# One-hot tiles made a step ahead, three-tile runs in the last block, and cleared-tile matmuls at the start of a DLRM tower kernel

## The reference, cut to what matters

```
e = jnp.stack([tbl_f[ids[:, f]] for f in range(39)], axis=1)      # [512, 39, 32]
p = e[:, ROW, :]; q = e[:, COL, :]                                # all pairs i < j
z = jnp.einsum('bpc,apc,bpa->bp', p, w, q)                        # [512, 741]
h = jnp.concatenate([z, dense_ctx], axis=1)
h = jnp.maximum(h @ W_top1 + b_top1, 0.0)                         # 757 -> 512
h = jnp.maximum(h @ W_top2 + b_top2, 0.0)                         # 512 -> 256
y = h @ W_top3                                                    # 256 -> 1
```

## Time and profile before

| | |
|---|---|
| time, median of three runs | 221.22 us (219.29 to 221.88) |
| time of the profiled execution | 221.21 us |
| its span, first to last instruction | 219.5 us |
| mean granted TensorE clock | 0.946 of full speed |
| TensorE busy | 194.5 us (89%), 1276 matmuls |
| VectorE busy | 143.3 us (65%), 140 instructions |
| GpSimd busy | 135.1 us (62%), gathers until 141 us |
| ScalarE busy | 41.8 us (19%) |
| transfers | 9.75 MB, nearly all in the first 28 us |

### The profile page before, as it was taken

One profiled execution on the slowest core, in us unless ns is written; L12 is line 12 of the kernel. 1 busy time (PEld: TensorE's weight loads), 2 busy tenths in 40 slices (PEclk: granted clock), 3 DMA queues, 4 the chain that ended last, 5 costly groups with the idle time before them and its releaser, 6 DMA issues.

```text
span 219.5 us, 3186 instructions
## 1 busy us (share of the span) xinstructions
PE 194.5 (89%) x1276; PEld 60.4 (28%) x1276; DVE 143.3 (65%) x140; ACT 41.8 (19%) x55; POOL 135.1 (62%) x202
## 2 busy tenths in 40 slices
PE   2599956568489999999998999999989999899895
PEld 1244512111122222232323232323322232222341
DVE  3599924743506889899967658899964566455310
ACT  3977820000020002001111021101011121101323
POOL 7998988898988888888888888600022222204000
PEclk9999996676758999999999999999999999999999
DMA  5999900000000000000000000000000000000000
GB/s 151 290 323 410 330 12 15 9 12 9 12 15 12 10 12 17 13 12 10 15 12 12 13 14 11 12 3 1 1 1 3 0 0 0 0 3 1 0 0 0
DMA packets 6682, 9.75 MB, mean 44 GB/s; under 512 B 1974, under 2 KB 4470, under 8 KB 6667
## 3 DMA queue, kind: packets, MB, share of 16 engines
q1 hardware_dynamic: 3722, 8.03, 11.2%
q0 software_dynamic: 2944, 1.51, 3.8%
HBM read 9.53 MB, written 0.00 MB: 43 GB/s over the span
## 4 chain that ended last, share of the span: by engine, by line
PE 87%; DVE 5%; ACT 4%; issue 3%; POOL 1%; DVEq 0%; POOLq 0%
PE ps L554 32%; PE ps L567 23%; PE ps L578 9%; PE ps L521 9%; PE ps L516 5%; PE ps L591 3%; DVE prod L475 3%; PE ps L532 2%; PE ps L502 2%; PE ps L586 2%; DVE hot L460 1%; ACT lower L403 1%; ACT ids_half L398 1%; PE ps L597 1%; ACT eT L412 1%
## 5 line engine op out<-in xcount | busy, mean ns | idle before, releaser
L475 DVE TENSOR_TENSOR prod<-ps,eT 128x1024 f32<-128x1024 f32 (+1 forms) x100 | 110.9, 1165 | 56.2 <-PE ps L554 46.3
L370 POOL DMA_INDIRECT gathered<-tbl,ids_sb x92 | 92.9, 1010 | 15.3 <-issue 15.0
L554 PE MATMUL ps<-eT,w_sb 32*128 32x512 f32 (+2 forms) x380 | 76.3, 663 | 2.6 <-ACT eT L413 1.5
L567 PE MATMUL ps<-prod,sel 128*32 128x512 f32 x380 | 53.5, 619 | 0.0
L384 POOL TENSOR_TENSOR tabs<-tabs 128x512 f32<-128x512 f32 x8 | 10.1, 1268 | 52.1 <-ACT tabs L433 52.1
L554 PEld LDWEIGHTS ps<-eT,w_sb 32*128 32x128 f32 (+2 forms) x380 | 23.9, 189 | 53.9 <-issue 34.4
L460 DVE TENSOR_SCALAR hot<-ids_half,row_of 125x2048 bf16<-125x2048 f16 x34 | 28.3, 899 | 4.1 <-ACT ids_half L398 4.1
L377 POOL MEMSET pause<- 128x256 f32 x91 | 30.3, 333 | 0.1
L516 PE MATMUL ps<-hot,tabs 125*32 125x512 bf16 x136 | 16.0, 456 | 12.5 <-DVE hot L460 10.3
L521 PE MATMUL ps<-hot,lower 125*32 125x512 bf16 x272 | 25.5, 455 | 0.0
L578 PE MATMUL ps<-z_sb,w_sb 128*128 128x512 f32 x40 | 20.3, 621 | 1.4 <-ACT eT L416 1.4
(11 more groups left out here) (30 smaller groups left out, 46.1 us busy)
## 6 DMA issues: line engine op xcount, KB each, us to landing
w_sb<-w SPq DMA_DIRECT2D x1, 1536.0 KB
gathered<-tbl,ids_sb POOLq DMA_INDIRECT x92, 2.3
tabs<-hot SPq DMA_DIRECT2D x3, 448.0 KB
w_sb<-wst SPq DMA_DIRECT2D x1, 640.0 KB, 13.1
w_sb<-wst SPq DMA_DIRECT2D x1, 576.0 KB, 11.9
tabs<-hot SPq DMA_DIRECT2D x1, 560.0 KB
w_sb<-wst SPq DMA_DIRECT2D x1, 512.0 KB, 10.4
w_sb<-w SPq DMA_DIRECT2D x1, 512.0 KB
```

Of the source, the lines that this page charges most:

```text
L370: pool.indirect_dma_start(gathered[J][:, b, K * r:K * r + K], None, tables[f], bass.IndirectOffsetOnAxis(ap=ids_sb[:, F * b + f:F * b + f ...
L475: dve.tensor_tensor(prod[:, p % XSLOTS, 0:n, :], ps[:, s:s + n, :], eT[:, I:I + 1, :].broadcast_to([P, n, B]), ALU.mult).then_inc(multipli ...
L554: mm = pe.matmul(ps[:, 2 * (p % TSLOTS) + i - first, :], w_sb[rows, w_tile(q), :], eT[rows, J, :], start=True, stop=True)
L567: mm = pe.matmul(z_ps[K * (u % G):K * (u % G) + K, :], sel[:, u // G, :], prod[:, p % XSLOTS, t - FIRST_TILE[p], :], start=(u < G), stop=( ...
```

## The change

Four things:

- **One-hot tiles a step ahead.** A new plan entry "hot" is what VectorE follows for one-hot tiles; "look" is TensorE's alone. The tiles of tables 0 to 2 stand at the same place as before. Table 3's first four tiles are made before quad 0, two more before quad 1's product, and so on; the looks are split 2, 2, 2 and 4 instead of 2, 3, 3 and 2.
- **Three-tile runs.** Pairs become runs: two tiles for full blocks, three in block 9, with banks 0 to 2 and 3 to 5 by turns, and product slots in threes of twelve single ones. Where runs of both lengths overlap, `run_ahead` finds the last earlier run that used one of the same banks or slots.
- **Cleared-tile matmuls.** VectorE first clears 32 partitions of `prod` (512 columns). TensorE multiplies that tile by itself, 256 columns, twice before its first wait for constants, and twice after the ids of table 1, once ScalarE has copied those of table 0. The results go to bank 2 and are used by nobody.
- Names and views of `prod` follow.

```diff
+TBANKS = 6
+XTILES = 12
+RUNS, RUN_BANK, RUN_SLOT = [], [], []
+for _q in range(NQUAD):
+    _n = 2 if FIELDS_IN[QUADS[_q][0]] == G else 3
+    for _i in range(0, QUADS[_q][2], _n):
+        _k = sum(FIELDS_IN[QUADS[_run[0]][0]] == FIELDS_IN[QUADS[_q][0]] for _run in RUNS)
+        RUNS.append((_q, _i, min(_n, QUADS[_q][2] - _i)))
+        RUN_BANK.append(_n * (_k % (TBANKS // _n)))
+        RUN_SLOT.append(_n * (_k % (XTILES // _n)))
...
+def run_ahead(p, at):
+    return max([i + 1 for i in range(p) if at[i] < at[p] + RUNS[p][2] and at[p] < at[i] + RUNS[i][2]], default=0)
...
-    steps += [("ids", 0), ("lower", 0), ("ids", 1), ("look", 0, 0, 3), ("lower", 1), ("ids", 2), ("look", 0, 3, 8),
-              ("keep", 0), ("lower", 2), ("ids", 3), ("look", 1, 0, 8), ("lower", 3), ("keep", 1), ("look", 2, 0, 8),
-              ("keep", 2), ("quad", 0), ("look", 3, 0, 2), ("quad", 1), ("look", 3, 2, 5), ("quad", 2),
-              ("look", 3, 5, 8), ("quad", 3), ("look", 3, 8, 10), ("keep", 4), ("keep", 3)]
+    steps += [("ids", 0), ("lower", 0), ("ids", 1), ("hot", 0, 0, 8), ("look", 0, 0, 3), ("lower", 1), ("ids", 2),
+              ("look", 0, 3, 8), ("keep", 0), ("lower", 2), ("ids", 3), ("hot", 1, 0, 8), ("look", 1, 0, 8),
+              ("lower", 3), ("keep", 1), ("hot", 2, 0, 8), ("look", 2, 0, 8), ("keep", 2), ("hot", 3, 0, 4),
+              ("quad", 0), ("look", 3, 0, 2), ("hot", 3, 4, 6), ("quad", 1), ("look", 3, 2, 4), ("hot", 3, 6, 8),
+              ("quad", 2), ("look", 3, 4, 6), ("hot", 3, 8, 10), ("quad", 3), ("look", 3, 6, 10), ("keep", 4),
+              ("keep", 3)]
...
 DVE:
+            dve.memset(prod[0:K, 0, :], 0.0).then_inc(warm_zeroed, 1)
...
-                if step[0] == "look":
+                if step[0] == "hot":
...
-                        if p >= XSLOTS:
-                            dve.wait_ge(summed, SUMS_THROUGH[p - XSLOTS])
+                        if run_ahead(p, RUN_SLOT):
+                            dve.wait_ge(summed, SUMS_THROUGH[run_ahead(p, RUN_SLOT) - 1])
...
 PE:
+            def keep_warm(bank, n):
+                zeros = prod[0:K, 0, :]
+                for _ in range(n):
+                    pe.matmul(ps[:, bank, 0:B // 2], zeros[:, 0:P], zeros[:, 0:B // 2], start=True, stop=True)
+
+            pe.wait_ge(warm_zeroed, 1)
+            keep_warm(2, WARM[0])
...
+                    if h == 1:
+                        pe.wait_ge(ids_half_made, 1)
+                        keep_warm(2, WARM[1])
...
-                        if p >= TSLOTS:
-                            pe.wait_ge(multiplied, p - TSLOTS + 1)
+                        if run_ahead(p, RUN_BANK):
+                            pe.wait_ge(multiplied, run_ahead(p, RUN_BANK))
```

More of the change, by code:

```diff
@@ L71 @@
 WTILES = W_BASE[NBLK]
[L74 to L80, removed]
+TBANKS = 6
[8 more added lines that the diff above has]
+        RUN_SLOT.append(_n * (_k % (XTILES // _n)))
+NRUN = len(RUNS)
+RUN_OF_TILE = [p for p, (_, _, n) in enumerate(RUNS) for _ in range(n)]
+FIRST_TILE = [TILE_BASE[q] + i for q, i, _ in RUNS]
+def run_ahead(p, at):
+    return max([i + 1 for i in range(p) if at[i] < at[p] + RUNS[p][2] and at[p] < at[i] + RUNS[i][2]], default=0)
 ZTILES = P // G
@@ L90 @@
 PAUSE = 256
+WARM = [2, 2]
 def sources(q):
@@ L183 @@
 EARLY = [s[1:] for s in PLAN if s[0] == "early"]
-SUMS_THROUGH = [next(i + 1 for i, s in enumerate(SUMS) if s[1] + s[2] >= FIRST_TILE[p] + PAIRS[p][2])
-                for p in range(NPAIR)]
+SUMS_THROUGH = [next(i + 1 for i, s in enumerate(SUMS) if s[1] + s[2] >= FIRST_TILE[p] + RUNS[p][2])
+                for p in range(NRUN)]
 assert sorted(TURNS) == list(range(NBLK))
@@ L223, in dlrm_tower @@
         w_sb = sb("w_sb", [P, WTILES, P])
-        prod = sb("prod", [P, XSLOTS, 2, B])
+        prod = sb("prod", [P, XTILES, B])
         row_int = {n: sb(f"row_int{n}", [P, n], I32) for n in ROW_SETS}
@@ L248, in dlrm_tower @@
         h_early = [tabs[:, M1 * B * i:M1 * B * (i + 1)].rearrange("p (m b) -> p m b", m=M1) for i in range(2)]
[L250 to L253, removed]
+        h1_sum = [prod[:, m, :] for m in range(M1)]
+        h1_sb = [prod[:, M1 + m, :] for m in range(M1)]
+        h2_sb = [prod[:, 2 * M1 + m, :] for m in range(M2)]
+        y_sb = prod[0:1, 2 * M1 + M2, :]
         ps = ctx.enter_context(nc.psum_tensor("ps", [P, 8, B], F32))
@@ L270, in dlrm_tower @@
         pad_zeroed = sem("pad_zeroed")
+        warm_zeroed = sem("warm_zeroed")
         rows_numbered = sem("rows_numbered")
@@ L464, in _ @@
                     J, I, _ = QUADS[q]
-                    for p in range(NPAIR):
-                        if PAIRS[p][0] != q:
+                    for p in range(NRUN):
+                        if RUNS[p][0] != q:
                             continue
-                        n = PAIRS[p][2]
+                        n = RUNS[p][2]
                         dve.wait_ge(t_made, p + 1)
@@ L471, in _ @@
                             dve.wait_ge(eT_made, turns(J))
-                        if p >= XSLOTS:
-                            dve.wait_ge(summed, SUMS_THROUGH[p - XSLOTS])
-                        s = 2 * (p % TSLOTS)
-                        dve.tensor_tensor(prod[:, p % XSLOTS, 0:n, :], ps[:, s:s + n, :],
+                        if run_ahead(p, RUN_SLOT):
+                            dve.wait_ge(summed, SUMS_THROUGH[run_ahead(p, RUN_SLOT) - 1])
+                        s, x = RUN_BANK[p], RUN_SLOT[p]
+                        dve.tensor_tensor(prod[:, x:x + n, :], ps[:, s:s + n, :],
                                           eT[:, I:I + 1, :].broadcast_to([P, n, B]), ALU.mult).then_inc(multiplied, 1)
@@ L545, in _ @@
                         pe.wait_ge(eT_made, turns(2))
-                    for p in range(NPAIR):
-                        if PAIRS[p][0] != q:
+                    for p in range(NRUN):
+                        if RUNS[p][0] != q:
                             continue
-                        _, first, n = PAIRS[p]
-                        if p >= TSLOTS:
-                            pe.wait_ge(multiplied, p - TSLOTS + 1)
+                        _, first, n = RUNS[p]
+                        if run_ahead(p, RUN_BANK):
+                            pe.wait_ge(multiplied, run_ahead(p, RUN_BANK))
                         for i in range(first, first + n):
                             rows = source_rows(q, i)
-                            mm = pe.matmul(ps[:, 2 * (p % TSLOTS) + i - first, :], w_sb[rows, w_tile(q), :],
+                            mm = pe.matmul(ps[:, RUN_BANK[p] + i - first, :], w_sb[rows, w_tile(q), :],
                                            eT[rows, J, :], start=True, stop=True)
@@ L558, in _ @@
                     for t in range(step[1], step[1] + step[2]):
-                        p = PAIR_OF_TILE[t]
+                        p = RUN_OF_TILE[t]
                         u = t % ZTILES
-                        if t == step[1] or p != PAIR_OF_TILE[t - 1]:
+                        if t == step[1] or p != RUN_OF_TILE[t - 1]:
                             pe.wait_ge(multiplied, p + 1)
@@ L567, in _ @@
                         mm = pe.matmul(z_ps[K * (u % G):K * (u % G) + K, :], sel[:, u // G, :],
-                                       prod[:, p % XSLOTS, t - FIRST_TILE[p], :],
+                                       prod[:, RUN_SLOT[p] + t - FIRST_TILE[p], :],
                                        start=(u < G), stop=(u >= ZTILES - G or t >= NTILE - G))
@@ L584, in _ @@
                     wait_z(pe, NZ - 1)
-                    pe.wait_ge(multiplied, NPAIR)
+                    pe.wait_ge(multiplied, NRUN)
                 pe.matmul(h1_ps[m], w1_sb[:, NZ - 1, P * m:P * m + P], z_sb[:, NZ - 1, :],
```

## The result

The changed kernel took 205.91 us in the median of four runs (205.15 to 208.18), the kernel before 221.55 on the same chip (219.29 to 224.46, four runs). The ratio is 0.934, 95% interval 0.922 to 0.946. The forecast was 205.8. The profiled execution took 205.15 us with a span of 203.4 us, against 221.21 and 219.5 before: 16.1 us less.

What follows compares the result with a forecast made beforehand. TensorE bounds the kernel, taking turns with VectorE's one-hot tiles. Of 20.6 us won early, 12.3 remain after block 7's gather wait; plus 3.1 from block 9, 15.4 off 221.2 gives 205.8 us, range 201.5 to 210.

Steps and rivals of the forecast that it cites:

- Part 1: Table 3's looks: one-hot tiles made ahead bring block 3's transposes 17.9 us earlier; 20.6 with the second gain.
- the second gain: From block 3's transposes on: the same work at the high clock level takes 5.8 instead of 8.4, 2.7 us more.
- The gathers: Block 7's rows land only at 102.0: TensorE idles 5.2 us, and 12.3 of 20.6 us remain at block 8.
- recovery: Behind block 7's wait: the clock is low after the idle, costing 2.7 us, bounds 0 and 4.
- Part 2: Cleared-tile multiplications at the start: table 0's looks 0 to 2 run at the high level, up to 1.5 us; sum 0.
- Part 3: Three-tile runs in block 9: 5.06 us saved on lone third tiles, less one new wait; net 3.1, bounds 1.2 and 5.1.
- new wait: Block 9, before quad 48: a three-tile product waits for a slot whose sums come late; TensorE waits 1.95 us, once.
- Rival 1: Block 7's wait: the clock stays up over it, 203.1 us; chance 0.17.
- rival 2: Gathers are not in the way because rows land earlier than read, 197.5 us; chance 0.06.
- rival 3: Early stage gains little: TensorE at half speed from 28.9 on, transposes move some 8 only; 208 to 211 us; chance 0.12.
- Rival 4: Beside table 3's tiles: a gather is held for each whole one-hot tile, 5.8 us more, 211.6 us; chance 0.03.
- rival 5: At block 8's transposes: GpSimd's gathers become the bound, slower than before; 227 us at 1.85 a step; chance 0.02.

Runs made afterwards that it cites:

- e1: Kernel before plus only one-hot tiles a step ahead (pairs in block 9, no cleared-tile matmuls), first chip: 256.8 us, before 262.8, ratio 0.975.
- e2: Kernel before plus only three-tile runs in block 9 (one-hot tiles made where looked up, no cleared-tile matmuls), first chip: 261.5 us, before 262.8.
- e3: Kernel before plus only the cleared-tile matmuls, first chip: 262.6 us, before 262.8, ratio 1.003.
- e10: e1 again on the third chip: 244.6 us, kernel before 251.5.
- e5: Changed kernel with GpSimd's pause memset behind each gather cut from 256 to 64 columns, second chip: 198.45 us, before 222.55, ratio 0.911.
- e7: Changed kernel plus nine unused matmuls before TensorE's wait for block 7's rows, second chip: 206.3 us, before 222.55, ratio 0.950.
- e0: Changed kernel again, unaltered, on the second chip: 210.0 us, kernel before 222.55.
- e11: e10 with GpSimd's pause cut from 256 to 64 columns, third chip: 314.7 us, before 251.5, ratio 1.252.
- e8: Changed kernel with the pause of 64 columns and block 9's runs starting at slots 6 to 8, third chip: 309.7 us, before 251.5, ratio 1.230.
- e6: Changed kernel with block 9's runs starting at product slots 6 to 8 instead of 0 to 2, second chip: 204.3 us, before 222.55, ratio 0.940.
- e4: Changed kernel without the cleared-tile matmuls, first chip: 249.7 us, before 262.8, ratio 0.953.

## Why the prediction was right, point by point

**Part 1.** Forecast: last look of table 3 ends 41.9, block 3's transposes at 43.4. Measured: 42.03 and 43.55. The pace was VectorE's as forecast. That it came out to 0.15 us is in part luck: table 2's looks ended at 29.24 and not at 28.9, so quad 0 started at 30.76 for 30.4 and VectorE's first product at 31.93 for 31.6; this was made good because two one-hot tiles took 1.42, 1.66 and 1.32 us until the next product started where the forecast had 1.65. VectorE's timeline:

```profile
33.07 1.50 DVE L477 TENSOR_SCALAR hot<-ids_half,row_of 125x2048 bf16<-125x2048 f16 x2
34.49 2.34 DVE L492 TENSOR_TENSOR prod<-ps,eT 128x1024 f32<-128x1024 f32 x2
36.75 1.74 DVE L477 TENSOR_SCALAR hot<-ids_half,row_of 125x2048 bf16<-125x2048 f16 x2
38.41 1.21 DVE L492 TENSOR_TENSOR prod<-ps,eT 128x1024 f32<-128x1024 f32 x1
39.54 1.40 DVE L477 TENSOR_SCALAR hot<-ids_half,row_of 125x2048 bf16<-125x2048 f16 x2
40.86 2.34 DVE L492 TENSOR_TENSOR prod<-ps,eT 128x1024 f32<-128x1024 f32 x2
```

From block 3's transposes to block 5's it is 21.1 us (64.66 - 43.55) instead of 24.0 (61.31 to 85.33), so the second gain, the clock, is 2.9 for 2.7 (granted 1.00 from 43.5 to 52.0, where it was 0.64 from 61.3 to 69.7). That part 1 carries it is shown by block 3's transposes in e1, e2 and e3 (above). Up to block 5 its size alone can be read in e10, which has nothing else: 67.78 for 85.33, 17.6 us, or 3.1 less than in the profile after, as its first six looks were slow, up to 19.03 (0.50 to 0.66 us on the upper matmuls, for 0.39). What part 1 alone takes off the whole time was never measured on an undisturbed chip.

**The gathers.** Forecast: rows of block 7 at 102.0, 5.2 us of wait, 2.7 of recovery, block 8 at 128.6. Measured: 101.56, 4.96, 2.8 (26.72 for 23.90), 128.28. Block 6 waited 0.17 for the 0.4 of the forecast. The three looks of before that the forecast took the low clock from have a granted clock of 0.50 (at 33.98, 0.62 us), 1.00 (at 48.97, 0.40 us) and 0.55 (at 57.09, 0.58 us); here it was 0.50 from 101.5 to 107.0. e5 shows that the wait and its recovery are the gather's doing. That the wait hides what is lost ahead of it shows for some 3 us, not for the 5 of the forecast, in e7 and e0: there block 3's transposes are 3 us later (46.6) than in the profile after, and still TensorE waits, 3.83 us in e0. But block 7's rows came 1.7 us later as well, which the forecast had held to be independent: in e0 one gather (at 18.71) took 1.83 us for 1.20 and those around it came late, at a time when VectorE's one-hot tiles waited for slow looks. That these waits are the cause is not shown.

**Part 2.** Forecast: worth 0 in the sum; so it was. The cost was read rightly: the two pairs end at 3.58 and 10.02, and the first look starts at 9.95 for 9.88. The gain was not: the first looks should have run at 0.39 and did not. In the profile after, the upper four matmuls of the first looks take 0.62 and 0.65, and the first look at 0.40 starts at 14.34, against 14.36 before. Over all traces it starts at 14.3 to 19.4 with the cleared-tile matmuls and at 14.4 to 19.0 without, in seven traces each. No trace shows that they bring the quick looks earlier. Nor does one show that a low clock makes the first looks slow: from 1.00 to 14.30 the granted clock is 1.00 in all fourteen, so the forecast's clock was the author's assumption here. What the slow looks cost, up to 3 us before block 3, is mostly hidden by the gathers anyway.

**Part 3.** Forecast: a three-tile product of 1.75, a new wait of 1.95 before quad 48, net 3.1. Measured: 1.754, 1.95, net 3.47. The 0.4 more comes from two places: from quad 49 to what follows quad 50 it is 1.92 us (173.20 to 175.12) for the 2.14 of the forecast, and the last ten sums take 2.77 where they took 2.99 before, which the forecast had left as it was; why they are shorter is not known. (The forecast's 1.07, 1.45 and 3.50 are from one start to the next; the lengths printed in the earlier trace rows are a little longer, 1.13 for 1.07.) Not in the sum was that the new wait can lower the clock, as in e0, e2 and e5: 1.6 to 3.2 us more.

**The sum.** 12.3 + 3.1 = 15.4 forecast, 12.59 + 3.47 = 16.06 in the profiled executions. The mechanism of each term of the sum was found as forecast, but that the median came within 0.1 us of 205.8 is luck: the profiled execution was 0.65 below the forecast, the others lie up to 208.18, and the same kernel had a median of 210.0, the edge of the range, on the second chip.

**The rivals.** Rival 1 fell with the slow transposes and early product behind the wait (1.11 and 3.78 us, granted 0.50), rival 2 with the wait itself (4.96), rival 3 with block 3's transposes at 43.55. Rival 4 had block 7's rows at 107.8; their last gather started at 99.29, and one of 1.30 us was the longest beside table 3's tiles. The 0.25 us by which a gather is longer beside a tile does not settle what rival 4 assumes, though: under it a gather that met only the last part of a tile would wait for that part alone, and no run tells the two apart. For rival 5 gathers would have had to come 1.76 us apart; they came 1.44 apart in most of the span.

## What to carry to other kernels

Before a stall is counted as a gain, ask of every producer with a pace of its own when it delivers: here 20.7 us were won up to block 5, and 8.1 of them were given back (12.6 left) at the first block whose gather could not be hurried, most of it as a wait and the rest as a low clock behind it. A buffer handed over between two runs of different length needs a look at who held it last; a shift of two slots took the wait away at no cost. And a change to the pace of gathers is to be tried on more than one chip, since the same edit took the changed kernel from 205.4 to 211.2 us down to 198.0 to 199.3 on one (e0, e5), and part 1 alone from 236.7 to 247.8 up to 314.3 to 315.4 on another (e10, e11).

## What the runs showed of the hardware that was not expected

**Gathers can hold the other engines back, on some chips.** On the third chip, with the short pause, TensorE's timeline of e8 in the looks, with nothing to wait for that the profile shows:

```profile
64.50 0.59 PE L548 MATMUL ps<-hot,lower 125*32 125x512 bf16 x1 [1.52 <-issue]
65.91 0.58 PE L548 MATMUL ps<-hot,lower 125*32 125x512 bf16 x1 [0.82 <-issue]
67.31 0.58 PE L548 MATMUL ps<-hot,lower 125*32 125x512 bf16 x1 [0.82 <-issue]
```

and GpSimd's at the same time:

```profile
63.44 0.95 POOL L386 DMA_INDIRECT gathered<-tbl,ids_sb  x1
64.55 0.15 POOL L393 MEMSET pause<- 128x64 f32 x1 [0.16 <-POOL pause L393]
64.85 0.95 POOL L386 DMA_INDIRECT gathered<-tbl,ids_sb  x1
65.96 0.15 POOL L393 MEMSET pause<- 128x64 f32 x1 [0.16 <-POOL pause L393]
66.26 0.95 POOL L386 DMA_INDIRECT gathered<-tbl,ids_sb  x1
```

Matmuls start 1.41 us apart and so do gathers, where the same looks run at 0.65 us for twelve matmuls otherwise. It begins at 16 us and ends with the gathers (the last starts at 130.2; from 133.5 on the matmuls of a look follow each other again, and from 137.6 a look starts every 0.65 us), and the intervals after it are those of the undisturbed kernel: 23.89 us from block 7 to block 8. With the pause of 256 columns it comes later and is milder: in e10 the transposes of block 5 are at 67.78, 21.11 us after block 3's as on the second chip, then block 6's come 26.5 us later instead of 13.8. Its TensorE timeline shows where it sets in:

```profile
67.78 0.66 PE L559 MATMUL ps<-ident,gathered 128*128 128x128 f32 x4
...
74.74 1.13 PE L581 MATMUL ps<-eT,w_sb 32*128 32x512 f32 x4 [1.19 <-issue]
76.08 1.69 PE L581 MATMUL ps<-eT,w_sb 32*128 32x512 f32 x4 [0.22 <-DVE prod L492]
```

On the second chip neither pause shows any of it: in e0, e5, e6 and e7 every idle of TensorE is ended by something that the profile shows. With the pause of 256 columns the first such stop past the looks is at 66.3 to 82.7 us in e1 to e4 and at 74.7 in e10; with 64 columns it is at 16.6 in e8 and e11. What it is, why it sets in earlier at the quicker pace, why the onset moves by 16 us between kernels with the same pause, and why chips differ, no run here tells.

**A lone tile costs what three cost**, 1.12 us against 1.13; two take as long (1.13 at 190.10 there), and so do four in the changed kernel (1.14 at 154.93).

**A wait of 1.95 us can lower the clock or not**: it did in e0, e2 and e5 (block 9's stage 39.76, 41.31, 39.71, granted clock over it 0.96, 0.92, 0.96), not in the profile after, e4 and e7 (38.12 and 1.00 in all three), with the same instructions around it.
